# Stores that land during the next stage, low-rank products moved forward, and four weight rows loaded a stage early, in a two-layer gated cross-attention kernel

## The chip, the cores and the metric

The kernel runs on 1 core of one Trainium2 chip. That core has five engines with instruction streams of their own, PE (TensorE), DVE (VectorE), ACT (ScalarE), POOL (GpSimd) and SP (SyncE), and 16 DMA engines. The engines wait for one another on semaphores alone. The metric is the device time of one execution in microseconds (us).

## The reference

Two layers of a gated block over x (16 batches of 128 rows, 1024 channels) and a context of the same shape. Cut to what matters:

```python
x = x + tanh(g_xattn[0]) * L0_xattn(layernorm(x), ctx, ctx, ...)   # 16 heads, 4 superposed parts each
x = x + tanh(g_ffn[0])   * L0_ffn(layernorm(x), ...)
x = x + tanh(g_xattn[1]) * L1_xattn(layernorm(x), ctx, ...)        # 8 heads, windows of 16 keys
x = x + tanh(g_ffn[1])   * L1_ffn(layernorm(x), ...)

def L0_xattn(q, k, v, ...):      # proj: y = x @ W.T + b; interfere mixes the 4 parts of a head
    qh, kh, vh = interfere(proj(q, Wq, bq)), interfere(proj(k, Wk, bk)), interfere(proj(v, Wv, bv))
    weights = softmax(einsum('bhqdm,bhkdm->bhqkm', qh, kh) / sqrt(dk), axis=3)
    return einsum('bhqkm,bhkdm->bhqdm', weights, vh) @ Wo.T + bo

def L0_ffn(x, W, bias, A, Bf, coeffs, scales):
    out = einsum('bsd,od->bso', x, W) + bias
    xa = einsum('bsd,erd->ebsr', x, A)              # 16 low-rank pairs of rank 16
    return out + einsum('ebsr,eor,e->bso', xa, Bf, coeffs * scales)
```

All is float32. The second layer's attention slides over windows; its FFN gates rows and columns by clusters.

## The kernel before

Six stages follow one another, each a block of instructions on all five engines: `project_q` (queries of layer 0), `project_kv` (its keys and values), `attention0` (attention, output projection and first residual), `ffn0_project1` (layer 0's FFN and layer 1's projections), `attend1_select` and `ffn1`. What one stage hands to the next goes through DRAM (q0, k0, v0, x1, x2, q1, k1, v1, x3, xT). A stage ends in this way: SP waits until the stage's last stores have landed (`sp.wait_ge(q_out[k], ...)` and the like), each engine runs to the end of its block, the stage's semaphores are cleared, and all engines meet in a barrier (`Stage.clear`, L78). Then the next stage's instructions begin; its SBUF tiles lie where the tiles of the stage before lay.

Products with a large weight run as three passes of float32r matmuls over a high and a low part: ACT copies a row block into `hi`, and another engine writes `lo` as the rest. A weight has 8 row blocks ("rows" 0 to 7, 128 x 1024, 512 KB each).

**Folded weights** (`FoldedWeight`: wq, wk, wv). SP loads a row into one of `RAW` = 4 raw slots (L118), PE multiplies it by the fold matrix (L126, 16 instruction records a row), ACT writes hi (L140), DVE lo (L147). A slot is loaded again when the fold of its row is done. In `project_kv` SP loads four rows of Wk, then the first 256 context columns `kv_cin` (1 MB, L493), then the other four.

**The low-rank weight** (`LowRankWeight`, `ffn0_project1`). The low-rank update is added to the weight once: PE computes a row of the product A·Bf (`product`, L176: 4 matmuls, 8 records, in one of two pairs of PSUM banks), DVE adds it to the loaded row (`add`, L184), ACT writes hi (L188), POOL lo (L192). A product of row r waits until `add` of row r-2 has freed its banks. PE's opening order is: products 0 and 1, the transposes of tile 0 (L850), then the wait for `xlo` of tile 0 (DVE's L772), and then for each of the eight chunks c: product c+2, and the three main matmuls of chunk c (L866), which wait for lo of row c. Then come the transposes of tile 1 and the loop over the 16 tiles. `staggered` writes out such loops: each part works some tiles ahead of the others.

**SP's queue** is in order: a DMA behind a wait is not issued until the wait is over. In `attention0` it issues the bias row `wo_gbias` (L1382), then the first queries and keys (L1391, L1393). DVE scales that bias before its first maximum (L1473, then L1478), and POOL waits for the scaled bias.

## Time and profile before

| what | us |
|---|---|
| three runs | 2136.23, 2137.4, 2142.19 (median 2137.4) |
| the profiled execution | 2138.3 |
| its span, first to last instruction | 2136.4 |
| PE busy | 1973.0 (92% of the span) |
| DVE, ACT, POOL busy | 1058.9, 657.7, 391.4 |
| mean granted TensorE clock | 0.958 of full speed |
| DMA | 328.67 MB, 154 GB/s over the span |

The chain that ended last names only `ffn1`, for it stops at the end of a stage. By the trace the barriers (L78) stand at 244, 651, 1172, 1500 and 1946 us. Times of an instruction are from the span's start. A wait in brackets at the end of a row is the idle time of the engine just before it, with what ended it.

### The profile page before, as it was taken

Reading aid. Unit: us, or ns where it says so; the run is one execution under the profiler, and the core shown is the slowest. Engines: PE = TensorE matmul, PEld = TensorE weight load, DVE = VectorE, ACT = ScalarE, POOL = GpSimd, SP = SyncE. Lnnn points to the kernel's source line nnn. Section 1 sums busy time; section 2 is a strip of 40 time slices with the busy share of each in tenths; the row PEclk is TensorE's granted clock in tenths of the full one; section 3 lists DMA queues with packets and bytes.
Section 4 is the critical chain, followed back from the end, with each engine's and each line's share of the span. In section 5 each row is a group of like instructions: output and inputs, shape, how many; then the busy total and the mean of one; then the engine's idle time right before and its main releaser. Section 6 shows DMA issues by size and latency. Waiting matters only on the chain. (4 is left out here: it accounts for less than half of the span.)

```text
span 2136.4 us, 50519 instructions
## 1 busy us (share of the span) xinstructions
PE 1973.0 (92%) x20126; PEld 1595.4 (75%) x20126; DVE 1058.9 (50%) x1858; ACT 657.7 (31%) x1114; POOL 391.4 (18%) x350
## 2 busy tenths in 40 slices
PE   7999799999995999999998899999599999986998
PEld 7999689999993777777776477777376767764887
DVE  5444231221112555555553455553788778854443
ACT  3222221111101443444443111112366666652000
POOL 0000000000005311111010300000565555630000
PEclk9999899999996999999999899999799999986999
DMA  4332444333347544455442345454755444413442
GB/s 152 119 118 98 180 139 182 127 136 117 122 155 299 200 179 183 181 217 208 184 162 72 142 168 187 179 186 157 208 152 146 130 131 126 137 71 129 147 142 85
DMA packets 149433, 328.67 MB, mean 154 GB/s; under 512 B 56432, under 2 KB 82672, under 8 KB 141104
## 3 DMA queue, kind: packets, MB, share of 16 engines
q1 hardware_dynamic: 147344, 326.04, 43.3%
q8 instruction: 110, 1.80, 0.4%
q10 hardware_dynamic: 1952, 0.60, 0.1%
q14 instruction: 27, 0.22, 0.0%
HBM read 200.25 MB, written 125.83 MB: 153 GB/s over the span
## 5 line engine op out<-in xcount | busy, mean ns | idle before, releaser
L1532 ACT ACTIVATE a_pt<-a_st_bank 128x1024 f32<-128x1024 f32 x128 | 131.2, 1025 | 268.5 <-PE a_st_bank L1578 268.5
L1070 POOL TENSOR_TENSOR a_sm<-a_sm,a_nmax 113x1024 f32<-113x1024 f32 x84 | 159.7, 1908 | 96.3 <-DVE a_nmax L1123 96.3
L1478 DVE TENSOR_REDUCE a_nmax<-a_s_bank 128x8 f32<-128x1024 f32 x128 | 156.6, 1223 | 27.5 <-PE a_s_bank L1566 21.0
L205 PE MATMUL kv_banks<-kv_ct_hi,wk_hi 128*128 128x256 f32 x512 | 146.2, 286 | 2.9 <-DVE wk_lo L147 2.9
L205 PE MATMUL q_qb<-q_xt_hi,wq_hi 128*128 128x256 f32 x512 | 145.5, 284 | 2.8 <-DVE wq_lo L147 2.8
L205 PE MATMUL kv_banks<-kv_ct_hi,wk_lo 128*128 128x256 f32 x512 | 145.6, 284 | 0.0
L205 PE MATMUL kv_banks<-kv_ct_lo,wk_hi 128*128 128x256 f32 x512 | 145.6, 284 | 0.0
L205 PE MATMUL q_qb<-q_xt_hi,wq_lo 128*128 128x256 f32 x512 | 144.9, 283 | 0.0
L205 PE MATMUL q_qb<-q_xt_lo,wq_hi 128*128 128x256 f32 x512 | 144.9, 283 | 0.0
L1248 PE MATMUL a_s_bank<-a_ks,a_qs 64*49 64x256 f32 x1344 | 96.9, 404 | 33.3 <-DMA a_ks<-k 13.2
L1117 DVE TENSOR_TENSOR a_sm<-a_s_bank,a_band 113x1024 f32<-113x1024 f32 x84 | 102.7, 1222 | 27.9 <-PE a_s_bank L1248 26.6
L1566 PE MATMUL a_s_bank<-a_ks,a_qs 64*128 64x128 f32 x1024 | 89.7, 297 | 22.4 <-DMA a_ks<-k 14.6
L866 PE MATMUL f_banks<-f_hi,f_xt_hi 128*128 128x512 f32 x256 | 106.7, 417 | 3.2 <-POOL f_lo L192 3.2
L1566 PEld LDWEIGHTS a_s_bank<-a_ks,a_qs 64*128 64x128 f32 x1024 | 71.2, 198 | 45.0 <-issue 37.7
L1123 DVE TENSOR_REDUCE a_nmax<-a_sm 113x16 f32<-113x1024 f32 x84 | 102.5, 1220 | 2.9
L825 ACT ACTIVATE f_shared<-f_banks,p_b 128x1024 f32<-128x1024 f32 x32 | 35.7, 1115 | 221.2 <-PE f_banks L882 221.2
L1183 ACT ACTIVATE a_probs<-a_sm 113x1024 f32<-113x1024 f32 x84 | 89.9, 1071 | 44.8 <-POOL a_sm L1070 44.8
L205 PE MATMUL kv_banks<-wv_hi,kv_ct_hi 128*128 128x512 f32 x256 | 100.4, 392 | 2.5 <-DVE wv_lo L147 2.5
L205 PEld LDWEIGHTS kv_banks<-kv_ct_hi,wk_hi 128*128 128x128 f32 x512 | 98.9, 193 | 3.4 <-DVE wk_lo L147 3.1
L866 PE MATMUL f_banks<-f_hi,f_xt_lo 128*128 128x512 f32 x256 | 101.4, 396 | 0.0
L866 PE MATMUL f_banks<-f_lo,f_xt_hi 128*128 128x512 f32 x256 | 101.3, 396 | 0.0
L1452 POOL TENSOR_TENSOR wo_xin<-wo_xin,wo_gbias 128x1024 f32<-128x1024 f32 x16 | 38.1, 2382 | 343.4 <-DMA wo_xin<-in_x 343.4
(209 smaller groups left out, 4587.0 us busy)
## 6 DMA issues: line engine op xcount, KB each, us to landing
a_qs<-q SPq DMA_DIRECT2D x32, 1024.0 KB, 5.5
a_ks<-k SPq DMA_DIRECT2D x32, 1024.0 KB, 7.2
k<-kv_raw SPq DMA_DIRECT2D x32, 512.0 KB
f_xin<-x SPq DMA_DIRECT2D x32, 512.0 KB, 4.5
a_vraw<-v SPq DMA_DIRECT2D x32, 304.0 KB
q_xin<-in_x SPq DMA_DIRECT2D x16, 512.0 KB, 6.3
q<-q_out_lo SPq DMA_DIRECT2D x16, 512.0 KB, 3.6
q<-q_out_hi SPq DMA_DIRECT2D x16, 512.0 KB, 4.2
```

The lines of the kernel that those rows point to most:

```text
L205: m = pe.matmul(out, a(x, c), b(y, c), start=(i + j == 0), stop=(len(terms) * j + i == n - 1))
L825: act.activation(halves(qk[j][:, s % 2, :]), pb, ACT.Identity, bias=b[:, j:j + 1]).then_inc(qk_done[j], 1)
L866: m = pe.matmul(gb[:, h, :], xt[x][:, s % 2, c, :], (w.hi, w.lo)[y][:, c, h * 512:h * 512 + 512], start=c == x == y == 0, stop=c == NC - 1 ...
L1070: pool.tensor_tensor(sm[live, k], sm[live, k], nmax[live, k, :].unsqueeze(2).to_broadcast([LIVE, 16, KEYS]), ALU.add).then_inc(shifted, 1)
L1117: dve.tensor_tensor(sm[live, k], scores, band[live].unsqueeze(1).to_broadcast([LIVE, 16, KEYS]), ALU.add).then_inc(added, 1)
L1123: dve.tensor_reduce(nmax[live, k, :], sm[live, k], X, ALU.max, negate=True).then_inc(maxed, 1)
L1183: act.activation(probs[live, k].rearrange("p c (h x) -> p (c h) x", h=2), sm[live, k], ACT.Exp).then_inc(expd, 1)
L1248: a = pe.matmul(to, qs[at, g % 2, t0:t0 + QT], ks[at, g % 2, :, t0:t0 + KEYS], start=True, stop=True, skip_group_check=True)
L1452: pool.tensor_tensor(xin[:, k, :], xin[:, k, :], gbias[:], ALU.add).then_inc(based, 1)
L1478: dve.tensor_reduce(to, s_bank[:].rearrange("p b (h x) -> p b h x", h=4), X, ALU.max, negate=True).then_inc(maxed, 1)
L1532: act.activation(pt[:, s % 2], st_bank[:].rearrange("p b (h x) -> p (b h) x", h=4), ACT.Exp).then_inc(expd, 1)
L1566: a = pe.matmul(s_bank[:, half, j * P:(j + 1) * P], qs[at, slot, 4 * (s % G) + j, :], ks[at, slot, 4 * (s % G) + j, :], start=True, stop=T ...
```

## The change

1. The waits for the last stores leave the ends of four stages: `project_q` (q_out), `project_kv` (v_out), `attention0` (out_sem) and `ffn0_project1` (x_out, v_out, qk_out). These semaphores are taken by `later`, so that no stage clears them before the last one does. The stage that reads or overwrites what is stored has the wait, in two parts: at its start for all but the last store of each semaphore, and some issues later for the last one. The wait for k_out stays. Some tiles are allocated in another order.
2. One raw buffer `e.raw` serves both projection stages. SP issues the loads of Wk's rows 0 to 3 in `project_q`, once all eight rows of Wq are folded; `project_kv` no longer issues them.
3. In `ffn0_project1` products 2 and 3 run ahead of PE's wait for `xlo`, and the others one chunk earlier. The lo parts of rows 6 and 7 go from POOL to DVE, with a semaphore of their own.
4. In `attention0` the load of `wo_gbias` is issued behind the first queries and keys.

```diff
@@ project_q
-        w = FoldedWeight(nc, ctx, e, "wq", e.i["Wq0"], sb("wq_raw", [P, RAW, D]),
+        w = FoldedWeight(nc, ctx, e, "wq", e.i["Wq0"], e.raw,
...
             load(1, 1, 0)
+            sp.wait_ge(w.folded, NC)
+            for r in range(RAW):
+                sp.dma_start(e.raw[:, r, :], e.i["Wk0"][r * P:(r + 1) * P, :]).then_inc(e.wk_loaded[r], 16)
             sp.wait_ge(unit_set, 1)
             sp.dma_start(e.k0[:, 0:32:16, 0, :], unit[:]).then_inc(unit_out, 16)
             staggered(sp, G, 2, [(2, load), (0, store)], started=(load,))
             sp.wait_ge(unit_out, 16)
-            for k in range(2):
-                sp.wait_ge(q_out[k], 64 * (G // 2) + START)
@@ project_kv
-            for r in range(RAW):
-                wk.load(sp, r)
             load(0, 0, 0)
             for r in range(RAW, NC):
                 wk.load(sp, r)
...
             sp.wait_ge(k_out, 160 * G + START)
-            for k in range(2):
-                sp.wait_ge(v_out[k], 16 * G + START)
@@ ffn0_project1
+            for k in range(2):
+                sp.wait_ge(e.x1_out[k], 16 * (B // 2 - 1) + START)
             load_x(0, 0, 0)
...
-            for r in range(3, NC):
+            for r in range(3, 6):
                 w.split_lo(pool, r)
...
             for r in range(3, NC):
                 w.add(dve, r)
+            for r in range(6, NC):
+                w.split_lo(dve, r)
...
             def product(h):
                 def run(t, s, i):
+                    if isinstance(t, int) and t + h == 0:
+                        w.product(pe, 2)
+                        w.product(pe, 3)
                     if h == 0:
                         pe.wait_ge(xlo, done(t))
...
-                        if opening and c + 2 < NC:
-                            w.product(pe, c + 2)
+                        if opening and 0 < c < NC - 3:
+                            w.product(pe, c + 3)
@@ attention0
-            sp.dma_start(gbias[:], e.i["bo0"].partition_broadcast(P)).then_inc(bias_in, 16)
+            for k in range(2):
+                sp.wait_ge(e.q_out[k], 64 * (B // 4) + START)
+                sp.wait_ge(e.v_out[k], 16 * (B // 2 - 1) + START)
...
             def load_weights(s):
+                if s == -15:
+                    sp.dma_start(gbias[:], e.i["bo0"].partition_broadcast(P)).then_inc(bias_in, 16)
+                if s == -12:
+                    for k in range(2):
+                        sp.wait_ge(e.v_out[k], 16 * (B // 2) + START)
```

The order of the instructions at two places. SP's queue from the last stores of `project_q` into `project_kv`, before; `q` stands for the stored queries, `kv_cin` for the context columns:

```order
L301 DMA q<-q_out_lo 32x4x1024
L301 DMA q<-q_out_hi 32x4x1024
L259 UNCONDITIONAL_BRANCH
L488 UNCONDITIONAL_BRANCH
L118 DMA kv_raw<-in_Wk 128x1024 x4
L493 DMA kv_cin<-in_ctxT 128x8x256
L118 DMA kv_raw<-in_Wk 128x1024 x4
L118 DMA kv_raw<-in_Wv 128x1024 x8
```

And now:

```order
L309 DMA q<-q_out_lo 32x4x1024
L309 DMA q<-q_out_hi 32x4x1024
L266 UNCONDITIONAL_BRANCH
L498 UNCONDITIONAL_BRANCH
L503 DMA kv_cin<-in_ctxT 128x8x256
L125 DMA raw<-in_Wk 128x1024 x4
L125 DMA raw<-in_Wv 128x1024 x8
```

Four loads of Wk have left the head of the stage; the context columns are its first transfer.

PE's opening of `ffn0_project1`, before (`f_lr_b`, `f_lr_a`: the low-rank factors; `f_rows`: the normalised tile; `f_hi`, `f_lo`: the weight):

```order
L176 MATMUL f_banks<-f_lr_b,f_lr_a 128x512 x8
L850 MATMUL f_banks<-ident_sb,f_rows 128x128 x8
L176 MATMUL f_banks<-f_lr_b,f_lr_a 128x512 x4
L866 MATMUL f_banks<-f_hi,f_xt_hi 128x512
L866 MATMUL f_banks<-f_lo,f_xt_hi 128x512
L866 MATMUL f_banks<-f_hi,f_xt_lo 128x512
L176 MATMUL f_banks<-f_lr_b,f_lr_a 128x512 x4
```

And now:

```order
L183 MATMUL f_banks<-f_lr_b,f_lr_a 128x512 x8
L857 MATMUL f_banks<-ident_sb,f_rows 128x128 x8
L183 MATMUL f_banks<-f_lr_b,f_lr_a 128x512 x8
L876 MATMUL f_banks<-f_hi,f_xt_hi 128x512
L876 MATMUL f_banks<-f_lo,f_xt_hi 128x512
L876 MATMUL f_banks<-f_hi,f_xt_lo 128x512
L183 MATMUL f_banks<-f_lr_b,f_lr_a 128x512 x4
```

One more product (4 matmuls) stands ahead of the first main matmul. On DVE two `L199 TENSOR_TENSOR f_lo<-f_shared,f_hi 128x1024` now follow the last `add` and stand ahead of the normalisation of tile 2; on POOL three instead of five follow the second root.

## Rows read from the trace of the kernel before

**Rows 1.** The page: span, and busy time of PE (share, instructions).

```profile
span 2136.4 us, 50519 instructions
PE 1973.0 (92%) x20126; PEld 1595.4 (75%) x20126; DVE 1058.9 (50%) x1858; ACT 657.7 (31%) x1114; POOL 391.4 (18%) x350
```

**Rows 2.** Waits of SP's queue for its last stores, by line of the wait.

```profile
SPq L314 <- DMA q<-q_out_hi: 3.6, 1, 3.6
...
SPq L739 <- DMA v<-p_v: 2.5, 1, 2.5
...
SPq L1428 <- DMA x<-wo_xin: 2.3, 1, 2.3
...
SPq L519 <- DMA v<-kv_raw: 2.3, 1, 2.3
```

**Rows 3.** Timeline (start, us, engine, line): end of `project_q`, start of `project_kv`.

```profile
238.46 1.21 SPq L301 DMA_DIRECT2D q<-q_out_hi  x1
244.99 1.78 SPq L118 DMA_DIRECT2D kv_raw<-in_Wk  x4
246.82 0.71 SPq L493 DMA_DIRECT2D kv_cin<-in_ctxT  x1
249.50 12.77 PE L126 MATMUL kv_banks<-fold,kv_raw 128*128 128x128 f32 x100 [14.16 <-DMA kv_raw<-in_Wk]
...
259.26 1.92 ACT L566 ACTIVATE kv_ct_hi<-kv_cin 128x2048 fp32r<-128x2048 f32 x1
```

**Rows 4.** Timeline of PE: the fold of Wq's last row.

```profile
33.75 2.05 PE L126 MATMUL q_tb<-fold,wq_raw 128*128 128x128 f32 x16 [0.81 <-DMA wq_raw<-in_Wq]
```

**Rows 5.** Stretch 40 to 50: busy per engine, clock, DMA share, GB/s.

```profile
40.00:50.00 10.00, 10.00 (x86) 10.00 (x85) 4.54 (x10) 1.43 (x3) 1.06 (x2) 1.00 0.01 2
```

**Rows 6.** Timeline: first transfers and first scores of `attention0`.

```profile
652.23 0.64 SPq L1391 DMA_DIRECT2D a_qs<-q  x1
...
655.70 0.75 DVE L1473 TENSOR_SCALAR wo_gbias<-wo_gbias,gate 128x1024 f32<-128x1024 f32 x1 [7.70 <-DMA wo_gbias<-in_bo]
...
661.88 1.12 PE L1566 MATMUL a_s_bank<-a_ks,a_qs 64*128 64x128 f32 x8 [14.60 <-DMA a_ks<-k]
```

**Rows 7.** Timeline of PE: the opening of `ffn0_project1`.

```profile
1173.83 8.85 PE L176 MATMUL f_banks<-f_lr_b,f_lr_a 128*128 128x512 f32 x16 [6.20 <-PEq L78]
...
1188.78 6.49 PE L176 MATMUL f_banks<-f_lr_b,f_lr_a 128*128 128x512 f32 x8 [5.22 <-DVE f_xt_lo L772]
...
1195.80 3.60 PE L176 MATMUL f_banks<-f_lr_b,f_lr_a 128*128 128x512 f32 x8
...
1216.84 0.50 PE L866 MATMUL f_banks<-f_hi,f_xt_hi 128*128 128x512 f32 x1
...
1220.95 0.50 PE L866 MATMUL f_banks<-f_hi,f_xt_hi 128*128 128x512 f32 x1 [3.16 <-POOL f_lo L192]
...
1221.77 1.91 PE L850 MATMUL f_banks<-ident_sb,f_rows 128*128 128x128 f32 x8
```

**Rows 8.** Timelines of DVE and POOL in the same opening.

```profile
1183.12 2.35 DVE L184 TENSOR_TENSOR f_shared<-f_banks,f_shared 128x1024 f32<-128x1024 f32 x2
...
1187.50 1.23 DVE L772 TENSOR_TENSOR f_xt_lo<-f_banks,f_xt_hi 128x1024 fp32r<-128x1024 f32 x1 [2.04 <-ACT f_xt_hi L831]
...
1195.37 1.22 DVE L184 TENSOR_TENSOR f_shared<-f_banks,f_shared 128x1024 f32<-128x1024 f32 x1 [6.65 <-PE f_banks L176]
...
1202.72 2.35 DVE L184 TENSOR_TENSOR f_shared<-f_banks,f_shared 128x1024 f32<-128x1024 f32 x2
...
1197.77 2.36 POOL L192 TENSOR_TENSOR f_lo<-f_shared,f_hi 128x1024 fp32r<-128x1024 f32 x1 [7.61 <-ACT f_hi L188]
```

**Rows 9.** Timeline of DVE in `ffn1`: six such subtractions of two SBUF tiles.

```profile
1952.97 6.89 DVE L1680 TENSOR_TENSOR f_lo<-f_raw,f_hi 128x1024 fp32r<-128x1024 f32 x6
```

**Rows 10.** Two stretches (columns as in rows 5).

```profile
1221.00:1225.00 4.00, 4.00 (x15) 3.51 (x16) 2.27 (x3) 1.02 (x1) 0.41 (x1) 0.59 0.00 0
...
690.00:700.00 10.00, 9.22 (x74) 6.71 (x72) 3.61 (x7) 3.35 (x6) 9.76 (x7) 0.53 0.55 215
```

More of the change, by code:

```diff
@@ L92, in scope, with later @@
     return sb, ps, sem
+def later(e, nc, name):
+    e.later.append(nc.alloc_semaphore(name=name))
+    return e.later[-1]
 def begin(eng, *sems):
@@ L108, in __init__ @@
         self.raw, self.banks = raw, banks
-        self.loaded = [sem(f"{name}_loaded{k}") for k in range(raw.shape[1])]
+        self.loaded = loaded or [sem(f"{name}_loaded{k}") for k in range(raw.shape[1])]
         self.folded = sem(f"{name}_folded")
@@ L270, in project_q @@
         mm = sem("q_mm"); qhi = sem("q_qhi"); qlo = sem("q_qlo")
-        q_out = [sem(f"q_q_out{s}") for s in range(2)]
+        e.wk_loaded = [later(e, nc, f"wk_loaded{r}") for r in range(RAW)]
+        q_out = e.q_out = [later(e, nc, f"q_q_out{s}") for s in range(2)]
         rep_mask = sb("rep_mask", [P, P]); perm = sb("perm", [P, P])
@@ L460, in project_kv @@
         sb, ps, sem = scope(nc, ctx)
-        raw = sb("kv_raw", [P, RAW, D])
+        raw = e.raw
         vout = raw[:, 0:2, :]
@@ L466, in project_kv @@
         kb, vb = banks[:, 0:4, :], banks[:, 4:8, :]
-        wk = FoldedWeight(nc, ctx, e, "wk", e.i["Wk0"], raw, [banks[:, 2 * k:2 * k + 2, :] for k in range(4)])
+        wk = FoldedWeight(nc, ctx, e, "wk", e.i["Wk0"], raw, [banks[:, 2 * k:2 * k + 2, :] for k in range(4)],
+                          loaded=e.wk_loaded)
         wv = FoldedWeight(nc, ctx, e, "wv", e.i["Wv0"], raw[:, 0:2, :], [vb[:, 0:2, :], vb[:, 2:4, :]])
@@ L472, in project_kv @@
         khi = sem("kv_khi"); klo = sem("kv_klo"); vmm = sem("kv_vmm"); vdone = sem("kv_vdone")
-        k_out = sem("kv_k_out"); v_out = [sem(f"kv_v_out{s}") for s in range(2)]
+        k_out = e.k_out = later(e, nc, "kv_k_out"); v_out = e.v_out = [later(e, nc, f"kv_v_out{s}") for s in range(2)]
         block = ctx.enter_context(nc.Block())
@@ L686, in ffn0_project1 @@
         vmm = sem("p1_vmm"); vdone = sem("p1_vdone")
-        x_out = [sem(f"f0_x_out{k}") for k in range(2)]; v_out = [sem(f"p1_v_out{k}") for k in range(2)]
-        qk_out = [[sem(f"p1_{c}_out{k}") for k in range(2)] for c in "qk"]
+        x_out = [later(e, nc, f"f0_x_out{k}") for k in range(2)]; v_out = [later(e, nc, f"p1_v_out{k}") for k in range(2)]
+        qk_out = [[later(e, nc, f"p1_{c}_out{k}") for k in range(2)] for c in "qk"]
+        e.f0_out = [*x_out, *v_out, *qk_out[0], *qk_out[1]]
         block = ctx.enter_context(nc.Block())
@@ L736, in _ @@
             staggered(sp, B, 4, steps, started=(load_x, load_ctx))
-            for k in range(2):
-                sp.wait_ge(x_out[k], 16 * (B // 2) + START)
-                sp.wait_ge(v_out[k], 16 * (B // 2) + START)
-                sp.wait_ge(qk_out[0][k], 16 * (B // 2) + START)
-                sp.wait_ge(qk_out[1][k], 16 * (B // 2) + START)
         @block.gpsimd
@@ L913, in attend1_select @@
         sb, ps, sem = scope(nc, ctx)
+        mark = sb("a_mark", [P, 1]); power = sb("se_power", [P, 1]); minus = sb("se_minus", [P, 1])
+        band = sb("a_band", [P, KEYS]); order = sb("a_order", [P, KEYS + QT])
+        seen = sb("se_seen", [P, NCL]); ones = sb("se_ones", [P, 1])
         qs = sb("a_qs", [P, 2, DPAD])
@@ L917, in attend1_select @@
         vpad = sb("a_vpad", [P, 2, NT1, 4, HD + 1])
-        band = sb("a_band", [P, KEYS]); order = sb("a_order", [P, KEYS + QT])
-        mark = sb("a_mark", [P, 1])
         sm = sb("a_sm", [P, 3, 16, KEYS])
@@ L975, in _ @@
             begin(sp, *x3_out, *xt_out)
+            for k in range(8):
+                sp.wait_ge(e.f0_out[k], 16 * (B // 2 - 1) + START)
             sp.wait_ge(pads[0], 2)
@@ L1022, in others @@
             def others(s):
+                if s == -15:
+                    for k in range(8):
+                        sp.wait_ge(e.f0_out[k], 16 * (B // 2) + START)
                 if s == -16:
@@ L1367, in attention0 @@
         x_in = [sem(f"wo_x_in{k}") for k in range(2)]; based = sem("wo_based"); summed = sem("wo_summed")
-        out_sem = [sem(f"wo_out{k}") for k in range(2)]
+        out_sem = e.x1_out = [later(e, nc, f"wo_out{k}") for k in range(2)]
         lr_in = sem("f0_lr_in"); lr_scaled = sem("f0_lr_scaled"); ce = sb("f0_ce", [P, 3, 2])
@@ L1419, in load_weights @@
             def load_weights(s):
+                if s == -15:
+                    sp.dma_start(gbias[:], e.i["bo0"].partition_broadcast(P)).then_inc(bias_in, 16)
+                if s == -12:
+                    for k in range(2):
+                        sp.wait_ge(e.v_out[k], 16 * (B // 2) + START)
                 r = s + NC
@@ L1426, in _ @@
             staggered(sp, N, 16, [(0, store), (16, load_half), (14, load_values), (6, load_x)], opening=load_weights)
-            for k in range(2):
-                sp.wait_ge(out_sem[k], 16 * (B // 2) + START)
         @block.gpsimd
@@ L1759, in attend1_select_ffn1 @@
         sb, ps, sem = scope(nc, ctx)
+        ctx.sems.extend(e.later)
         raw = sb("f1_raw", [P, NC, D])
@@ L1770, in program @@
     e = Env()
-    e.i = ins
+    e.i, e.later = ins, []
     dram = lambda name, shape, dt=F32: nc.dram_tensor(name, shape, dt).ap()
```

28 lines of the change are left out of this document (15 added, 13 removed).

## The prediction

> **What bounds the kernel now.** I read the page first: PE is busy for 1973.0 of 2136.4 us [rows 1], so PE is the bound, and a change that leaves its work alone can win only from its idle time, 163 us, and from stretches at the lower clock. Then I read PE's waits. The two longest do not come from the loops but from the heads of stages: 14.60 us for the first keys of `attention0` [rows 6], 14.16 us for the first row of Wk [rows 3]. Then SP's own waits: ahead of each of the four barriers it sits 3.6, 2.3, 2.3 and 2.5 us until the last store has landed, 10.7 us together [rows 2]. In these times no other engine has work left, so they are on the path. Last I read the timelines around the barriers. The reader is to see there which instruction PE starts with and what it waits for, since that decides whether an earlier barrier is an earlier start.
>
> **Part 1: the four landing waits.** Each barrier comes as much earlier as SP's wait was long, if nothing else is late. Other engines are not: at the end of `project_q` SP's last issue ends at 238.46 + 1.21 = 239.67 [rows 3], and it is the last to arrive in either kernel. The new waits in the next stage ask at their first place for stores that landed a tile earlier, and at their second place, some issues on, for the last one, which by [rows 2] lands 2.3 to 3.6 us after its issue; the barrier alone takes 244.99 - (239.67 + 3.6) = 1.7 us of that. Behind the second wait in `attention0` stand the second pair of query and key loads and all later loads, so a store that lands late would hold them up; I take nothing for it.
>
> **At `project_q` to `project_kv`** (part 2 belongs here). The barrier comes 3.6 us earlier. Before, SP issues the first load of Wk at 244.99, and PE's fold begins at 249.50 [rows 3]. With rows 0 to 3 already there PE starts as it does in `ffn0_project1`, where its first matmul runs at 1173.83 with the barrier as its releaser [rows 7] and no transfer to wait for. I put its start 0.4 us behind SP's first issue, an estimate. So the fold would begin at 244.99 + 0.4 - 3.6 = 241.8, a gain of 7.7 us. Is something late next? Rows 4 to 7 are requested when the folds of rows 0 to 3 are done. A row is 16 records, and 100 took 12.77 us [rows 3]: 2.0 us a row, so row 4's fold is due 8.2 us after row 0's began. Its load is issued 2.0 us after that beginning, which leaves 6.2 us; the first of four loads took 4.5 us to land (244.99 to 249.50), and now 1 MB of context is ahead of it. ACT took the context at 259.26, 9.8 us after the first fold; now it is issued first of all, at 241.4, and is due at 251.6. So I take the whole 7.7. Bounds: 4.7 if the 1 MB ahead of row 4 makes it 3 us late, 8.1 if PE starts together with SP. The four loads themselves are issued at about 36 us and their 2 MB fall in a stretch with a DMA share of 0.01 [rows 5]; what SP has behind them, the unit store and the tiles of the third pair, has 20 us of room. They leave the transfers ahead of Wq's last row fewer, whose wait was 0.81 us [rows 4]: 0.4 us, between 0 and 0.8. If that free stretch were not free, four loads would delay a tile load, and the cover is the 20 us just named.
>
> **At `project_kv` to `attention0`.** The barrier comes 2.3 us earlier. The first queries are issued at 652.23, 0.4 us of that spent on the bias issue in front, and PE starts at 661.88 [rows 6]. Moving the bias row (512 KB) behind the keys takes its bytes off the path to the first score, but DVE scales it (0.75 us) before its first maximum, and PE's second score waits for that maximum. The bytes are needed by then in either order. So the start of the score gains more and the second score less: 2.3 + 0.4 for the issue + 0.5 for the 2 MB coming first, - 0.75 for the scaling that now stands behind the keys = 2.5 us. Bounds: 1.0 (the last value store, still in flight, shares the DMA engines with the first loads, and the bias is over 1 us late) and 4.0 (the first keys come sooner by the whole 655.70 - 651.8 = 3.9 us that the bias took to land).
>
> **At `attention0` to `ffn0_project1`.** The barrier gives 2.3 us. Part 3: before, PE stands 5.22 us for `xlo` of tile 0, until 1188.78, and then 3.16 us for POOL's lo of the last row [rows 7]. Now product 2 needs only the first of the two adds of rows 0 and 1, done at 1183.12 + 2.35/2 = 1184.3 [rows 8]. A product with its three main matmuls takes (1216.84 - 1195.80)/5 = 4.2 us [rows 7], 3.4 and 0.8. So products 2 and 3, chunk 0, product 4 and chunk 1 end at 1184.3 + 3 x 3.4 + 2 x 0.8 = 1196.1. Product 5 needs add 3, and that stands behind DVE's normalisation of tile 1, whose root stands on POOL behind lo of row 2: `xlo` ends at 1188.7; from add 2's start to lo's start it was 1197.77 - 1195.37 = 2.4 us, lo takes 2.36, and from its end to add 3 it was 1202.72 - 1200.13 = 2.6, with the add 1.2 [rows 8]: 1188.7 + 2.4 + 2.36 + 2.6 + 1.2 = 1197.3. A wait of 1.2 us. Products 5 to 7 with chunks 2 and 3 end at 1197.3 + 11.8 = 1209.1. Then add and hi (2.4 as above) and lo on DVE (6.89/6 = 1.15 [rows 9] instead of 2.36 on POOL), with 0.3 for handovers, beside which chunks 4 to 6 run: chunk 7 starts at 1213.0 and the transposes of tile 1 at 1213.8, against 1221.77: 8.0 us. What DVE carries more, 2.3 us, lies in this chain; behind it come the normalisation of tile 2 and `xlo` of tile 1, about 6 us after 1213, and PE has transposes and 24 main matmuls to run until about 1220. Cover enough by 1 us.
> The clock adds to it. Right behind the 3.16 us wait the stretch 1221 to 1225 shows 0.59 of full clock, thus mostly 1.2 instead of 2.4 GHz [rows 10]. The transposes took 1.91 us there, and with the main matmuls behind them it is 1.5 us. That the pauses left, 1.2 and about 1.5 us, no longer let the clock fall is not shown, so I count 0.8. The Trainium skill, "TensorE: Matmul & The Clock Gate", section "HAM oscillation — how this bites in real kernels", says that a short wait between bursts of matmuls is paid again as a cold start of the next burst; the trace agrees for 3.16 us. By that rule in full, for shorter pauses too, the 0.8 would be a loss of up to 1.5.
> Together 2.3 + 8.0 + 0.8 = 11.1. Bounds: 0 (the landing wait goes, and the two subtractions on DVE come on the path with nothing gained by order) and 14.3 (PE runs all of 6 x 4.2 + 2 x 0.8 = 26.8 us from 1184.3 without a wait, and the whole 1.5 of the clock).
>
> **At `ffn0_project1` to `attend1_select`.** 2.5 us: SP, DVE and POOL start with memsets that move along with the barrier, and the first scores follow. Bounds 2.0 and 2.7.
>
> **Sum.** 0.4 + 7.7 + 2.5 + 11.1 + 2.5 = 24.2 us. The loops behind each head are PE's own work and keep their length. The profiled execution took 2138.3 us: 2138.3 - 24.2 = 2114.1. The median of the runs is 0.9 below the profiled one, so 2113.2 to 2114.1: I say 2114.
>
> **Rivals.**
> A. The landing waits are only moved: the new waits, or the first loads behind stores in flight, hold the next stage as long as before. For it: PE's head waits end with a DMA at two of four places [rows 3, 6]. Against it: SP was idle in those 10.7 us, and transfers could have been issued. All 10.7 lost: 2124.8.
> B. Rows 4 to 7 of Wk come late behind the context columns and the last query stores. For it: 6.2 us of room against 4.5 with 1 MB ahead. Against it: ACT and DVE take the context in between and give 2 us. 3 us lost: 2117.
> C. In the opening of `ffn0_project1` the chain over DVE, ACT and POOL is longer than I add it up. For it: four engines pass each row on, and two rows change theirs. Against it: its durations are rows. 5 us lost: 2119.
> D. Slower. The clock: in `attention0` PE stays at the low clock long after its first score; 690 to 700 still shows 0.53 [rows 10]. If the earlier, thinner start kept it low longer: product 2 took 6.49 us where the same work at full clock took 3.60 [rows 7], so each us at the low clock costs 0.45. From 24.2/0.45 = 54 us more of it the kernel is slower; with 70 us it would take 2114.1 + 0.45 x 70 = 2145.6. Against it: PE's busy share in the head is set by the same chain as before.
> E. No change, with A, B and C together and the DVE chain on the path: 24.2 - 10.7 - 3 - 8 = 2.5, thus 2136.
>
> **How the numbers follow.** Forecast 0.65, A 0.07, B 0.10, C 0.12, D 0.03, E 0.03. The measurement of this kernel tells 0.3% (6.4 us) from no change. A, B, C and the forecast lie below 2131: faster 0.94; E: same 0.03; D: slower 0.03. The forecast's own bounds add up to 7.7 and 29.9 us, which needs every term at one end; half of that on each side gives 2110 to 2122, and with B and C inside and A at the edge I take 2109 to 2122.
>
> **What would show it.** SP's waits for the last stores are gone from its list, and no wait of over 1 us stands at the new places. PE's first fold of Wk starts about 6.5 us after its last query matmul and its wait is for the barrier, not for a transfer; a wait for Wk in the middle of the folds is B. PE's first score of `attention0` comes about 2.5 us or more sooner after the barrier's old place, with DVE's scaling of the bias behind it. In `ffn0_project1` the wait before product 2 is under 1 us instead of 5.22, the transposes of tile 1 start some 40 us after the first product instead of 47.9, and the wait for POOL's last lo is gone. The prediction is wrong if the loops differ in length, or if one stage's gain is less than half its term.

## The result, and the profile after

The changed kernel takes **2106.3 us** (median of 4 runs, 2103.48 to 2106.68), the kernel before 2136.82 beside it (2134.7 to 2142.19): a ratio of 0.9851, interval [0.983, 0.9871], thus 30.5 us faster. The forecast was 2114.0 with a range of 2109 to 2122. The sign and the places were right; the gain was 6 us larger than the sum of 24.2, and outside the range.

The page of the profile after, its span and PE's row, as [rows 1] of before:

```profile
span 2104.9 us, 50557 instructions
PE 1963.7 (93%) x20126; PEld 1592.8 (76%) x20126; DVE 1060.7 (50%) x1860; ACT 657.0 (31%) x1114; POOL 386.6 (18%) x348
```

PE runs the same 20126 matmuls, but is busy for 9.3 us less. That is the first sign that the change did more than take waits away.

SP's waits for transfers, after (us in total, times, longest):

```profile
SPq L1424 <- DMA x<-wo_xin: 5.4, 8, 2.2
...
SPq L1056 <- DMA xT<-se_xt: 2.0, 1, 2.0
...
SPq L1693 <- DMA out<-f_out: 1.8, 1, 1.8
```

The four waits of [rows 2] are gone, and nothing of their kind stands at the new places: every wait for a DMA that is left was there before or belongs to the end of the kernel.

The timeline from `project_q` to `project_kv` after, as [rows 3]:

```profile
239.77 1.05 SPq L309 DMA_DIRECT2D q<-q_out_hi  x1
242.43 0.42 SPq L503 DMA_DIRECT2D kv_cin<-in_ctxT  x1
246.38 5.87 SPq L125 DMA_DIRECT2D raw<-in_Wk  x4
...
242.60 16.44 PE L133 MATMUL kv_banks<-fold,raw 128*128 128x128 f32 x128 [6.12 <-PEq L78]
...
252.90 1.91 ACT L572 ACTIVATE kv_ct_hi<-kv_cin 128x2048 fp32r<-128x2048 f32 x1
...
261.97 0.39 PE L212 MATMUL kv_banks<-kv_ct_hi,wk_hi 128*128 128x256 f32 x1 [2.93 <-DVE wk_lo L154]
```

PE's first fold waits 6.12 us, for the barrier and no longer for a transfer (14.16 before), and all 128 folds run in one piece of 16.44 us: rows 4 to 7 of Wk were there in time.

The start of `attention0` after, as [rows 6]:

```profile
640.24 0.63 SPq L1409 DMA_DIRECT2D a_qs<-q  x1
...
641.57 0.44 SPq L1439 DMA_DIRECT2D wo_gbias<-in_bo  x1
...
650.09 0.76 DVE L1494 TENSOR_SCALAR wo_gbias<-wo_gbias,gate 128x1024 f32<-128x1024 f32 x1 [11.55 <-DMA wo_gbias<-in_bo]
...
648.13 1.11 PE L1587 MATMUL a_s_bank<-a_ks,a_qs 64*128 64x128 f32 x8 [10.32 <-DMA a_ks<-k]
652.03 1.12 PE L1587 MATMUL a_s_bank<-a_ks,a_qs 64*128 64x128 f32 x8 [2.78 <-DVE a_nmax L1499]
```

The wait for the first keys is 10.32 us instead of 14.60. The scaling of the bias now ends after them (650.09 + 0.76), and the second score waits 2.78 us for the maximum behind it (1.32 before).

The opening of `ffn0_project1` after, PE and then DVE, as [rows 7] and [rows 8], and the clock of two stretches, as [rows 10]:

```profile
1159.56 9.70 PE L183 MATMUL f_banks<-f_lr_b,f_lr_a 128*128 128x512 f32 x16 [4.24 <-PEq L78]
...
1170.46 7.13 PE L183 MATMUL f_banks<-f_lr_b,f_lr_a 128*128 128x512 f32 x16 [0.33 <-DVE f_shared L191]
...
1183.33 3.70 PE L183 MATMUL f_banks<-f_lr_b,f_lr_a 128*128 128x512 f32 x8 [0.92 <-DVE f_shared L191]
...
1197.80 0.51 PE L876 MATMUL f_banks<-f_hi,f_xt_hi 128*128 128x512 f32 x1 [1.13 <-DVE f_lo L199]
...
1199.82 1.04 PE L857 MATMUL f_banks<-ident_sb,f_rows 128*128 128x128 f32 x8
```

```profile
1182.06 2.35 DVE L191 TENSOR_TENSOR f_shared<-f_banks,f_shared 128x1024 f32<-128x1024 f32 x2
...
1196.53 2.43 DVE L199 TENSOR_TENSOR f_lo<-f_shared,f_hi 128x1024 fp32r<-128x1024 f32 x2
```

```profile
1183.00:1200.00 17.00, 15.30 (x44) 8.04 (x45) 8.43 (x11) 5.28 (x5) 7.06 (x3) 1.00 0.00 1
1200.00:1204.00 4.00, 4.00 (x23) 3.41 (x22) 3.22 (x7) 1.03 (x1) 0.55 (x1) 1.00 0.00 0
```

Waits of 0.33, 0.92 and 1.13 us are what remains of 5.22 and 3.16. The transposes of tile 1 start 40.3 us after the first product (47.9 before), and the stretch around them has the full clock where 0.59 stood in [rows 10].

Cutting PE's stream at the same matmuls in both traces gives the length of each piece (us):

| piece of PE's stream | before | after | difference | predicted |
|---|---|---|---|---|
| start to first main matmul of `project_q` | 38.61 | 38.27 | -0.3 | -0.4 |
| `project_q`, main matmuls | 196.72 | 198.20 | +1.5 | 0 |
| its end to the first fold of Wk | 14.16 | 6.12 | -8.0 | -7.7 |
| folds | 18.84 | 19.37 | +0.5 | 0 |
| `project_kv`, main matmuls | 378.94 | 375.83 | -3.1 | 0 |
| its end to the first transposed score (L1599) | 33.53 | 30.71 | -2.8 | -2.5 |
| `attention0` from there | 486.83 | 486.80 | 0.0 | 0 |
| its end to the first projection of `ffn0_project1` (L892) | 67.81 | 56.31 | -11.5 | -11.1 |
| `ffn0_project1` from there | 259.70 | 256.42 | **-3.3** | 0 |
| its end to the first score of `attend1_select` | 13.15 | 10.93 | -2.2 | -2.5 |
| `attend1_select`, first score to the first of its six closing matmuls (L1338) | 431.95 | 428.88 | **-3.1** | 0 |
| from there to the last matmul of `ffn1` | 190.11 | 190.01 | -0.1 | 0 |
| behind PE's last matmul, to the end of the span | 6.0 | 7.0 | +1.0 | 0 |

The five predicted terms together are 24.9 us against 24.2. The rest of the gain stands in the rows whose forecast was 0: the loop of `ffn0_project1`, `attend1_select`, and small differences of both signs in the first two stages. The last row belongs to a cost of the change that the forecast has no term for (below, "What the forecast left out"). All rows together are the 31.5 us by which the span is shorter.

### The profile page after: what moved, and what is told of

The parts are those of the page before. It is cut to its first block and busy times, and to the rows that moved or that the text cites. A ratio compares the mean times of both kernels' runs of the same rounds, so it can differ in the third digit from the quotient of the medians.

```text
span 2104.9 us, 50557 instructions
## 1 busy us (share of the span) xinstructions
PE 1963.7 (93%) x20126; PEld 1592.8 (76%) x20126; DVE 1060.7 (50%) x1860; ACT 657.0 (31%) x1114; POOL 386.6 (18%) x348
## 5 line engine op out<-in xcount | busy, mean ns | idle before, releaser
L212 PEld LDWEIGHTS q_qb<-q_xt_hi,wq_hi 128*128 128x128 f32 x512 | 99.0, 193 | 3.0 <-issue 3.0
```

What stands on the lines that cost most here:

```text
L212: m = pe.matmul(out, a(x, c), b(y, c), start=(i + j == 0), stop=(len(terms) * j + i == n - 1))
```

## The experiments

Each kernel is after or before with one edit. A ratio is against runs of before beside it. "Loop" is the piece of `ffn0_project1` in the table, "period" the time between its tiles.

**1. Is it the place of the weights?** The diff moves the line that makes `LowRankWeight` up behind `f0_shared`, ahead of the other buffers. The compiled programs show what this does: `f0_hi` starts at byte 147200 of each partition before, a multiple of 64, and at 66784 after, 32 past one; `f0_lo` follows it. After, with those two moved by 32 bytes and all else left in its place:

```diff
+        sb("f0_pad0", [P, 8])
         w = LowRankWeight(nc, ctx, e, "f0", e.i["WfT0"], shared, banks[:, 4:8, :])
+        sb("f0_pad1", [P, 8])
```

> The changed kernel with a tile of 32 bytes a partition ahead of the low-rank weight and one behind it: f0_hi and f0_lo start 32 bytes later (at 66816 and 99584, multiples of 64; before at 147200, a multiple of 64; in the changed kernel 66784, no such multiple), all tiles behind them 64 bytes later. Theory P1 (the start address of the weight's parts against 64 bytes sets the pace of their 512-column matmuls): the step between main matmuls goes from 0.227 back to 0.233 us, the period of a tile in the loop from 17.06 to 17.29 us, and the kernel is about 3.5 us slower than the changed one: 2109.8. Rival P2 (the region of SBUF in which they lie): the period stays 17.06, 2106.3. Rival P3 (the new opening order sets the loop's pace): 17.06 as well.

Measured: 2112.62 us (2108.62 to 2113.06), ratio 0.9885 [0.9867, 0.9902], period 17.27 us, loop 259.5. Its matmuls, and those of before and after, in equal stretches of the loop (count, busy time, mean ns of one). Before, after, experiment 1:

```profile
L866 PE MATMUL f_banks<-f_hi,f_xt_lo 128*128 128x512 f32 x189 | 74.7, 395 | 0.0
```

```profile
L876 PE MATMUL f_banks<-f_hi,f_xt_lo 128*128 128x512 f32 x193 | 75.5, 391 | 0.0
```

```profile
L878 PE MATMUL f_banks<-f_hi,f_xt_lo 128*128 128x512 f32 x190 | 75.1, 395 | 0.0
```

395 ns before, 391 after, 395 again with 32 bytes in front. From start to start it is 0.2332, 0.2284 and 0.2330 us in the mean (the matmuls overlap). The region of the buffer and the order of the lines did not change: 32 bytes make the difference. The median is 6.3 us above after's, of which the loop explains 3.1; the rest is within what medians of four runs of one kernel do here (experiment 4 is after itself and spans 2101.59 to 2112.13).

**2. The same from the other side.** Before, with only the allocation of the weight moved to where after has it:

```diff
         shared = sb("f0_shared", [P, 8, D])
+        banks = ps("f0_banks", [P, 8, 512])
+        w = LowRankWeight(nc, ctx, e, "f0", e.i["WfT0"], shared, banks[:, 4:8, :])
...
-        banks = ps("f0_banks", [P, 8, 512])
-        w = LowRankWeight(nc, ctx, e, "f0", e.i["WfT0"], shared, banks[:, 4:8, :])
```

> The kernel before with one edit: the low-rank weight is allocated right behind f0_shared, as in the changed kernel (66784 instead of 147200); no wait, order or load is changed. P1 and P2: the loop's period is 17.06 instead of 17.29 us, 3.3 to 3.6 us faster than before: 2133.3. P3: 17.29, 2136.8. In the second attention the tiles lie as before: if the 3.1 us that it gained is chance of the clock, its length falls anywhere between the two; if it belongs to the change, it stays at that of before (369.7 us from the first scores to the last small product).

Measured: 2134.45 us (2130.66 to 2137.46, 12 runs), ratio 0.9983 [0.9974, 0.9993], period 17.06, loop 256.42, as in after. This move alone, with no instruction changed, is worth 3.3 us of the loop and 1.5 to 5.6 of the median.

**3. The landing waits back.** After, with the four removed waits at the ends of the stages again, and the new ones kept:

```diff
             sp.wait_ge(k_out, 160 * G + START)
+            for k in range(2):
+                sp.wait_ge(v_out[k], 16 * G + START)
```

(and likewise for `q_out`, `out_sem` and `e.f0_out`)

> The changed kernel with the four waits for the last stores put back at the ends of their stages; everything else stays. Theory S (each barrier comes as much earlier as SP waited): slower than the changed kernel by 3.6 + 2.3 + 2.3 + 2.5 = 10.7 us, 2117.0, with 3.6 of it between the last query matmul and the first fold. Rival M (the waits were moved, not removed): under 3 us slower.

Measured: 2117.82 us (2116.91 to 2118.42), ratio 0.9908 [0.989, 0.9926], 11.5 above after. Its waits:

```profile
SPq L325 <- DMA q<-q_out_hi: 4.1, 1, 4.1
SPq L753 <- DMA v<-p_v: 2.5, 1, 2.5
SPq L1457 <- DMA x<-wo_xin: 2.3, 1, 2.3
SPq L529 <- DMA v<-raw: 2.3, 1, 2.3
```

They sum to 11.2 us, and the four pieces behind them are longer than in after by 4.0, 2.1, 2.7 and 2.6: 11.4. What SP waited there was on the path to the full, and rival A falls. This kernel keeps the semaphores of `later` and what clearing them costs, so the 11.4 are the price of the waits alone.

**4. The changed kernel again,** with no edit.

> The changed kernel once more, for the chance in the lengths of the loops. If the short stretches at the lower clock inside the loops are chance: the query stage's loop has another length than 198.2 us (196.7 without the stretch that followed its first pause), and the second attention's 368.1 us differ by a us or two; the time lies in 2103 to 2107. If they belong to the program: the same stretches at the same places.

Measured: 2106.29 us (2101.59 to 2112.13), ratio 0.9861 [0.9837, 0.9884]. In its trace the heads behind the barriers repeat after's within 0.3 us, but the first main matmul of `project_q` comes at 36.85 instead of 38.27, `project_q` takes 196.70 instead of 198.20 and `attend1_select` 427.69 instead of 428.88, with the same program.

**5. The products forward alone.** Before with part 3 only:

```diff
+                    if isinstance(t, int) and t + h == 0:
+                        w.product(pe, 2)
+                        w.product(pe, 3)
...
-                        if opening and c + 2 < NC:
-                            w.product(pe, c + 2)
+                        if opening and 0 < c < NC - 3:
+                            w.product(pe, c + 3)
```

(and the subtractions of rows 6 and 7 on DVE)

> Before with the opening of ffn0_project1 alone changed: products 2 and 3 in front of tile 0's main matmuls, the subtractions of rows 6 and 7 on DVE; barriers, allocation and the rest as before. Theory S (the prediction's term): 8.0 us from the order and 0.8 from the clock, measured in after as 11.5 less a barrier wait of 2.3 = 9.2, so a median of 2128 and the tile period of ffn0 still 17.28 us, since the weights lie where they lay. Rival C (the chain through DVE, ACT and POOL is longer, and the earlier barrier paid for it): 4 us or less, 2133.

Measured: 2129.42 us (2124.45 to 2133.21, 6 runs), ratio 0.9961 [0.9947, 0.9975], thus 5 to 11 us. The opening takes 58.11 us, 9.7 less than before. PE in it:

```profile
1183.61 7.13 PE L176 MATMUL f_banks<-f_lr_b,f_lr_a 128*128 128x512 f32 x16 [0.86 <-DVE f_shared L184]
...
1196.48 3.70 PE L176 MATMUL f_banks<-f_lr_b,f_lr_a 128*128 128x512 f32 x8 [0.91 <-DVE f_shared L184]
...
1210.96 0.50 PE L871 MATMUL f_banks<-f_hi,f_xt_hi 128*128 128x512 f32 x1 [1.11 <-DVE f_lo L192]
```

The waits of 0.91 and 1.11 us are after's 0.92 and 1.13: the order makes this term by itself. Experiment 3, which has the order but not the earlier barrier, gives much the same from the other side: 67.81 - 59.02 = 8.8 us against before, and 67.01 - 59.02 = 8.0 against experiment 2, which has the weight's new place too. The period is 17.28 and the loop 259.70, as in before.

**6. Without the early load of Wk.** After with rows 0 to 3 loaded at the head of `project_kv`:

```diff
-            sp.wait_ge(w.folded, NC)
-            for r in range(RAW):
-                sp.dma_start(e.raw[:, r, :], e.i["Wk0"][r * P:(r + 1) * P, :]).then_inc(e.wk_loaded[r], 16)
...
+            for r in range(RAW):
+                wk.load(sp, r)
             load(0, 0, 0)
```

> After without the early loads: the first four rows of Wk are loaded behind the barrier at the head of project_kv, in front of the context, into the same buffer. Theory S: PE's first fold waits for a transfer again, 4.1 to 4.5 us; the span from the last query matmul to the first fold goes back by that much, and Wq's last row comes 0.3 us sooner: 2110.5. Rival (the barrier was the price, not the transfer; or the context now comes later and holds the keys too): under 1 us, 2107, or over 7 us, 2113 and more.

Measured: 2112.76 us (2110.99 to 2117.11), ratio 0.9877 [0.986, 0.9894]. First transfer and first fold:

```profile
242.65 1.83 SPq L125 DMA_DIRECT2D raw<-in_Wk  x4
...
247.68 14.50 PE L133 MATMUL kv_banks<-fold,raw 128*128 128x128 f32 x102 [11.14 <-DMA raw<-in_Wk]
```

The wait is 5.0 us longer than after's 6.12, and the folds take 1.0 us more, since row 4 comes later. With experiment 3's 4.0 us for the store it comes to 9.0, where the two together gave 8.0: each, taken back alone, costs a little more than the 3.6 and 4.1 I gave it.

**7. The bias row in front again.**

```diff
+            sp.dma_start(gbias[:], e.i["bo0"].partition_broadcast(P)).then_inc(bias_in, 16)
...
-                if s == -15:
-                    sp.dma_start(gbias[:], e.i["bo0"].partition_broadcast(P)).then_inc(bias_in, 16)
```

> After with the 512 KB bias row of attention0 loaded again in front of the first queries. Theory S: the order of the bias is worth 0.2 us to the second score (2.81 measured, 2.3 of it the barrier): 2106.5 with the first score itself 1 to 2 us later. Rival (the bias order is most of the term): 2 us or more, 2108.5.

Measured: 2109.06 us (2107.14 to 2112.54), ratio 0.9865 [0.9847, 0.9883]; the medians are 2.8 apart and the intervals overlap. The trace is finer: the first score waits longer and the second less.

```profile
652.54 1.11 PE L1586 MATMUL a_s_bank<-a_ks,a_qs 64*128 64x128 f32 x8 [12.57 <-DMA a_ks<-k]
654.97 1.12 PE L1586 MATMUL a_s_bank<-a_ks,a_qs 64*128 64x128 f32 x8 [1.32 <-DVE a_nmax L1498]
```

12.57 - 10.32 = 2.25 us lost at the first score, 2.78 - 1.32 = 1.46 gained at the second: 0.8 net, where I had 0.2.

**8. The buffers of `attend1_select`.** The diff also reorders them, which moves most of them by 32 bytes modulo 64. Before with that order alone:

```diff
+        mark = sb("a_mark", [P, 1]); power = sb("se_power", [P, 1]); minus = sb("se_minus", [P, 1])
+        band = sb("a_band", [P, KEYS]); order = sb("a_order", [P, KEYS + QT])
+        seen = sb("se_seen", [P, NCL]); ones = sb("se_ones", [P, 1])
         qs = sb("a_qs", [P, 2, DPAD])
...
-        band = sb("a_band", [P, KEYS]); order = sb("a_order", [P, KEYS + QT])
-        mark = sb("a_mark", [P, 1])
```

> Before with only the order changed in which attend1_select asks for its buffers, as after has it; every instruction as before. attend1_select took 431.95 us from its first score to its last matmul in before and 428.88 in after, where the 5292 small value matmuls over a_pt and a_vpad took 61.2 instead of 63.8 us. Theory P (placement): those take 61.2 us again and the stage 429 or less, 2.5 us and the median near 2134.3. Rival K (clock alone: the stage falls differently into low stretches): value matmuls 63.8, stage 432, median 2137.

Measured: 2137.16 us (2132.91 to 2143.08, 12 runs), ratio 0.9996 [0.9984, 1.0007]; stage 430.19 us, value matmuls 62.2. Neither theory is met: the stage lies between. The times of the value matmuls were a poor witness: each holds one or two steps of over 1 us, and without these they are 59.6 us in before, 59.0 in after and 59.5 in experiment 8. The runs side by side decide more. With before's places it took 431.95, 431.74, 428.51 and 430.86 us (before, experiments 2, 5, 13), with after's 425.91 to 430.90 over eleven traces, experiment 8 among them. Three stretches from first score to last matmul (PEclk is the number behind POOL's): before, after, experiment 1.

```profile
1508.30:1940.20 431.90, 388.73 (x8344) 283.22 (x8344) 320.45 (x550) 257.23 (x400) 237.06 (x212) 0.93 0.46 134
```

```profile
1479.00:1907.90 428.90, 387.50 (x8345) 282.60 (x8345) 320.32 (x550) 256.78 (x400) 236.80 (x212) 0.93 0.44 135
```

```profile
1480.00:1906.00 426.00, 382.95 (x8339) 279.19 (x8339) 321.64 (x545) 256.45 (x399) 237.52 (x217) 0.94 0.45 138
```

The spread within one arrangement, 5 us, is larger than the 3.1 to be explained, and the shortest has the highest clock. The clock records of the traces say more: in this stage 63.3 us of before stand at the lower level and 56.8 of after. Half of each is lost, if PE's work fills them: 31.7 and 28.4, a difference of 3.2 us, so in this pair the clock accounts for the 3.1. Whether the change took part in that is another question, and one trace of each kernel can't answer it.

**9 to 12. Which start counts?** Four kernels, each after with one pair of buffers wrapped in 32-byte pads as in experiment 1, and named here by that pair.

`wo_hi`, `wo_lo` of `attention0`:

> After with 32 bytes in front of and behind wo_hi and wo_lo in attention0, so that these two weights start at a multiple of 64 bytes (before and after: 32 bytes past one); its matmuls over 512 columns follow each other in 0.233 us there, as in ffn0_project1 of before. Theory R (a start at a multiple of 64 costs 0.006 us per matmul, whatever the kernel): attention0's step stays 0.233 or grows to 0.239, and the 0.233 it has already comes from elsewhere. Rival: the step falls to 0.227 and attention0 gets up to 4 us shorter, thus it is the place relative to other data and not the multiple of 64 that counts.

`f0_xt_hi`, `f0_xt_lo`, the 128-column operands:

> After with only f0_xt_hi and f0_xt_lo, the 128-column operands of ffn0_project1, moved by 32 bytes to a multiple of 64; f0_hi and f0_lo stay 32 bytes past one. Theory R (only the start of the 512-column operand counts): tile period stays 17.06 us, 2106.5. Rival D (what counts is whether both operands of a matmul start alike): period 17.28 us, 2110.

`f1_hi`, `f1_lo` of the last stage:

> After with f1_hi and f1_lo, the weights of the last stage, moved by 32 bytes to a multiple of 64. Theory R: their step goes from 0.227 to 0.233 us, the last stage takes 3.3 us more (256 x 3 main matmuls and a little), 2109.7. Rival (the effect belongs to ffn0_project1 alone): 0.227 and 2106.4.

`wo_xt_hi`, `wo_xt_lo`:

> After with only wo_xt_hi and wo_xt_lo, the 128-column operands of attention0's output matmuls, moved by 32 bytes to a multiple of 64; the weights stay 32 bytes past one. Theory R: step stays 0.233 us, 2106.5. Rival D (both operands' starts relative to each other): the step changes to 0.227, the stage up to 4 us shorter.

Measured, in this order: 2106.05 us (ratio 0.9869 [0.985, 0.9887]), 2111.6 (0.9879 [0.9856, 0.9901]), 2109.22 (0.9877 [0.986, 0.9893]), 2108.38 (0.9866 [0.9847, 0.9885]). The rows: experiment 10; then `ffn1` in after and in experiment 11; then `attention0` in after, 9 and 12.

```profile
L878 PE MATMUL f_banks<-f_hi,f_xt_lo 128*128 128x512 f32 x189 | 74.7, 395 | 0.0
```

```profile
L1769 PE MATMUL f_gb<-f_hi,f_xt_lo 128*128 128x512 f32 x228 | 70.2, 389 | 0.0
```

```profile
L1771 PE MATMUL f_gb<-f_hi,f_xt_lo 128*128 128x512 f32 x222 | 69.9, 396 | 0.0
```

```profile
L1640 PE MATMUL wo_gb<-wo_hi,wo_xt_lo 128*128 128x512 f32 x204 | 64.3, 396 | 0.0
```

```profile
L1642 PE MATMUL wo_gb<-wo_hi,wo_xt_lo 128*128 128x512 f32 x204 | 64.3, 396 | 0.0
```

```profile
L1642 PE MATMUL wo_gb<-wo_hi,wo_xt_lo 128*128 128x512 f32 x202 | 63.8, 397 | 0.0
```

Experiment 10 refutes its theory R: the weights stay where after has them, only their partner moves to a multiple of 64, and the pace is before's, period 17.29 and loop 259.69. The rival that stands beside it holds: it is the two starts relative to each other. Experiment 11 shows it in another stage, 389 to 396 ns; a tile goes from 10.88 to 11.20 us and the stage from 176.5 to 181.0, where 3.3 us were expected. `attention0` doesn't care: 396 ns with equal starts and with unequal ones. Something else sets the pace there, and no run says what.

**13. Both at a multiple of 64.** Before with pads around `f0_xt_hi` and `f0_xt_lo`:

> Before with f0_xt_hi and f0_xt_lo moved by 32 bytes, so that in ffn0_project1 the weights and the 128-column operands both start at a multiple of 64 bytes; nothing else is changed. Theory D (equal starts modulo 64 make the pace): the tile period falls from 17.28 to 17.06 us with before's weights where they are, 3.3 us, median 2133.5. Rival (both operands have to start 32 bytes past a multiple): 17.28, or more, and 2137.

Measured: 2135.78 us (2131.89 to 2141.12, 10 runs), ratio 0.9992 [0.9979, 1.0004], which by itself can't be told from no change; but the period is 17.10 us and the loop 256.99, against 17.28 and 259.70.

```profile
L868 PE MATMUL f_banks<-f_hi,f_xt_lo 128*128 128x512 f32 x192 | 75.5, 393 | 0.0
```

| start modulo 64: weights, partner | kernels | mean ns, f_hi by f_xt_lo | period | loop |
|---|---|---|---|---|
| 0, 32 | before, experiments 1, 5 and 8 | 395 | 17.27 to 17.28 | 259.5 to 259.7 |
| 32, 0 | experiment 10 | 395 | 17.29 | 259.7 |
| 0, 0 | experiment 13 | 393 | 17.10 | 257.0 |
| 32, 32 | after, experiment 2 and all others | 391 | 17.06 | 256.4 |

What the two starts do to each other inside the chip is left open: the runs show the step, not its reason.

**14. Everything alike.** After with gaps in seven places, so that the two operands of every frequent matmul start alike:

```diff
+GAPS = ("ident_sb", "gate", "p1_bvb", "a_qs", "a_pt", "a_att", "se_x2")
...
     def sb(name, shape, dt=F32):
+        if name in GAPS:
+            ctx.enter_context(nc.sbuf_tensor(f"{name}_gap", [P, 8], F32))
```

> After with 32-byte gaps in seven places, so that the two operands of every frequent matmul start alike modulo 64 bytes: the identity with what it transposes, p1_cin and p1_xn with p1_wt, a_pt with a_vpad, a_att_t with se_wt. Theory T (the effect is one of matmuls over 512 columns at one pass per column): nothing measurable, 2106.3, attend1_select 425 to 429 us. Rival U (every matmul pays it): 0.006 us for each of some 1300 matmuls of 128 and more columns, 8 us, 2098; it would beat after.

Measured: 2107.92 us (2102.2 to 2109.92), ratio 0.9865 [0.9847, 0.9884]; `attend1_select` 426.42. Nothing measurable, as theory T has it. No kernel here is measurably faster than after.

## Why the prediction was right and where it was wrong

**The landing waits** (10.7 us predicted): right for the waits. Experiment 3 gives 11.5. That SP's wait is path when no other engine has work left was the reading that carried it.

**Wq's last row** (0.4 us): not measured. The profiled pair has 0.3, but that piece takes 36.7 to 38.6 us over the sixteen traces, 38.27 and 36.85 in two of after itself and 38.34 in experiment 6, which has no early loads. That 0.3 looks like 0.4 is luck.

**Wk's first load** (4.1 us): right, slightly low. Experiment 6 gives 5.0 at the first fold and 6.0 to the end of the folds. The rows behind them were in time (one piece of 128 folds), so rival B falls.

**The start of `attention0`** (2.5 us): right, measured 2.8; of it 2.1 by the barrier (experiment 3) and 0.8 by the order of the bias (experiment 7), which I had at 0.2.

**The opening of `ffn0_project1`** (2.3 + 8.0 + 0.8): right. The piece gained 11.5, and the order 8.8 by experiment 3 and 9.7 by experiment 5. The two waits I forecast as 1.2 and about 1.5 us are 0.92 and 1.13, so rival C falls, and the transposes of tile 1 came 40.3 us after the first product, where "some 40 us" stood. But the parts of the 11.1 were off in both directions: PE's wait at the barrier shrank by 2.0 us (6.20 to 4.24) for 2.3, since the clearing ahead of it takes 0.5 longer, the transposes of tile 1 came 7.7 us sooner for 8.0, and from there to the first projection it is 1.9 us less for 0.8. That the total fits is in part luck. The last one is mostly the clock, of which I had counted half: in before's trace 3.4 us at half clock follow the wait of 3.16, 1.7 lost, and in after's none. The stretches behind those two waits show 1.00, which is 2.4 GHz. I had cited the Trainium skill, "TensorE: Matmul & The Clock Gate", section "HAM oscillation — how this bites in real kernels": by its rule carried over to such short waits this term would have been a loss of up to 1.5 us. The trace of after doesn't agree with that reading for waits of about 1 us; before's 0.59 stood behind one of 3.16. That reading was mine: the example in that section has waits of 3 to 5 us.

**The last head** (2.5 us): 2.2, right; the wait alone gave 2.6 (experiment 3), and a clearing that is 0.4 longer took the rest back.

**What the forecast left out** is the price of `later`. Ahead of each barrier POOL clears the semaphores of the stage. Before and after, the durations in ns:

```profile
L77 POOLq EVENT_SEMAPHORE_RANGE_CLEAR  x7: 69/225/312, 244.3 to 2136.0; - x7
```

```profile
L77 POOLq EVENT_SEMAPHORE_RANGE_CLEAR  x24: 44/70/142, 241.6 to 2104.5; - x24
```

That is 7 instructions against 24; experiment 3 has 24, experiments 2 and 5, without `later`, have 7. The compiled programs show why: one instruction clears a range of numbers, 99 to 133 for the first stage before; after it is 99 to 118 and 125 to 137, and the six numbers between belong to the kept `wk_loaded` and `q_out`. From the first clear to SP's release the traces have 0.46, 0.38, 0.49, 0.52, 0.55 and 0.80 us at the six ends before, and 0.62, 0.34, 0.96, 0.96, 1.18 and 1.82 after: 2.7 us more in all. So the waits less this price are worth some 11.4 - 2.7 = 8.7 us, an estimate from these two numbers. Whether semaphores taken in another order give the 2.7 back is not tested.

**Rival D** of the prediction, a clock that stays low for longer in `attention0`, falls too: the clock records have PE back at full clock 38.8 us behind its first score, and 37.6 us before.

**The step that failed** is the sentence "The loops behind each head are PE's own work and keep their length." Their work is the same, instruction for instruction, but not its pace. The diff moves two allocations. In `ffn0_project1` this puts the weights 32 bytes past a multiple of 64, as their partner is, and each main matmul over 512 columns starts 0.005 us sooner behind the one before: with 48 of them in a tile 0.22 us a tile, over 15 tiles the 3.3. Experiments 1, 2, 10 and 13 tie 3.3 us to that. I had read those lines of the diff as bookkeeping, though loops of another length were among my own signs of a wrong prediction. With this term the forecast would have been 2110.7, inside the range; what took the result out of it are, in the profiled pair, mostly lengths that the same sentence held fixed and that the clock moved: 3.1 us in `attend1_select` and 1.1 in the first two stages.

**Not settled** is whether the change has a part in the rest of the miss. In the profiled pair the rest is 3.1 us in `attend1_select` and 1.1 net in the first two stages, less the 1.0 behind PE's last matmul, which is part of the 2.7 above. The first two stages' loops take one of few lengths, from run to run: `project_q` 196.7 in before and in experiments 3, 4, 5, 8, 9 and 14, 198.0 to 198.2 in after and in seven others, 199.4 in experiment 12. Experiment 4 is after itself, so the 1.5 us are no effect of the change. For `project_kv` the case is weaker: 378.9 to 379.0 in all five traces that have before's head, 375.8 in five of the eleven that derive from after, 377.4 to 380.1 in the other six; an earlier start of the folds may take part in it. The clock over that stage, before and after:

```profile
268.30:647.30 379.00, 376.44 (x2432) 345.32 (x2432) 78.25 (x118) 52.41 (x87) 0.00 (x0) 0.99 0.38 138
```

```profile
262.00:637.80 375.80, 373.31 (x2432) 342.75 (x2432) 78.21 (x118) 52.29 (x87) 0.00 (x0) 1.00 0.38 138
```

The same 2432 matmuls, 0.99 against 1.00: before has two stretches of 3.4 us at 1.2 GHz, at 269.4 and 310.4, and after has none; half of them is the 3.1 us and a little. The first lies right behind a wait that after has as well, as its row at 261.97 shows. PE's first main matmul and the stretch from it, before:

```profile
268.34 0.39 PE L205 MATMUL kv_banks<-kv_ct_hi,wk_hi 128*128 128x256 f32 x1 [2.94 <-DVE wk_lo L147]
...
268.30:273.30 5.00, 4.96 (x29) 4.96 (x30) 0.00 (x0) 0.30 (x1) 0.00 (x0) 0.66 0.27 111
```

and the stretch after:

```profile
262.00:267.00 5.00, 5.00 (x43) 5.00 (x44) 0.48 (x1) 0.55 (x2) 0.00 (x0) 1.00 0.20 82
```

So the same wait, 2.94 and 2.93 us, was followed by the lower clock in one trace and by the full clock in the other. In `project_q` it is the other way round: its first main matmul waits 2.8 us in both, and 3.4 us at 1.2 GHz follow in after alone. In `attend1_select`, where the clock accounts for the pair's 3.1 us (experiment 8), the mean over before's arrangement is 430.8 us (4 traces) and over after's 428.2 (11), but experiment 8, timed in 12 runs, allows anything from 3.4 us faster to 1.5 slower.

**The range** was too narrow below. It was made from the terms' own bounds, all of them about heads, and left nothing for pieces that I took as fixed. Half of the way to the upper bound, 29.9 us, gives 2111 and not the 2110 that stands there; the 2109 taken was wider than that and still too high.

## What to carry to other kernels

Read an edit of allocations as an edit of the time: look up where the operands of the long matmul loops start, before and after. In loops of 512-column float32r matmuls like those of `ffn0_project1` and `ffn1`, keep the two of a pair alike modulo 64 bytes. A wait of the queue engine for its last stores was worth its whole length here, at four places where every other engine was done; no run tests the case where one is not. Count what the barrier costs in the same look: keeping semaphores past their stage made the clearing longer by 2.7 us. When a forecast holds a loop fixed, give the loop a spread of its own, taken from several traces of one kernel, and look in the clock records before calling a difference of 2 or 3 us an effect.

## What the runs showed of the hardware

- Matmuls of fp32r over 512 columns follow each other in 0.227 to 0.228 us in the mean when both operands start 32 bytes past a multiple of 64, and in 0.233 when one does and the other doesn't (`ffn0_project1` in the sixteen traces, and `ffn1` in experiment 11 against after); both at a multiple is a shade slower than both at 32 past (17.10 and 17.06 us a tile). In `attention0` the same kind takes 0.233 in the mean in either case. The Trainium skill, "SBUF — State Buffer", section "Operand start alignment", asks only for a multiple of the element size and says that this is about legality and not speed; for speed on TensorE these runs show that 32 bytes matter in these two stages.
- Clearing semaphores ahead of a barrier has a price by the instruction: with 7 of them in six places it is 3.2 us from the first clear to SP's release, with 24 it is 5.9 (before and after).
- Where the chip's clock is low in a long stage differs between two runs of one program: 1.5 us in `project_q` and 1.2 us in `attend1_select` (after and experiment 4); over eleven traces with the same code and places in `attend1_select` the stage's length spans 5 us.
- A wait of 2.9 us of PE in `project_kv` was followed by 3.4 us at 1.2 GHz in before and by none in after; waits of 0.9 and 1.1 us in `ffn0_project1` were followed by the full clock.
